# Cross-attention and a mixture of experts on one core: VectorE's order in attention, the top-four in wide operations, and an activation copy ahead of a sigmoid

## What is computed

```python
q = ctx @ Wq.T + bq; k = ctx @ Wk.T + bk
attention = softmax(q @ k.T)
x = x + layernorm(x) @ attention.T
h = layernorm(x)
top, idx = top_k(h @ gate_w.T + gate_b, 4)
weight = softmax(top)
gate = minimum(h @ w_gate[e] + b_gate[e], 7)
up = clip(h @ w_up[e] + b_up[e], -7, 7)
act = (up + 1) * gate * sigmoid(1.702 * gate)
x = x + sum(weight * (act @ w_down[e] + b_down[e]))
```

## Time and profile before

| | |
|---|---|
| median of 3 runs | 3115.03 us |
| the profiled execution | 3116.04 us, span 3113.9 us |
| TensorE matmuls busy | 2948.7 us, 95% of the span |
| VectorE busy | 1716.4 us, 55% |
| ScalarE busy | 1178.8 us, 38% |
| GpSimd busy | 563.5 us, 18% |
| mean granted TensorE clock | 0.984 of full speed |
| first gate product of the experts | 720.08 us |

### The profile page before, as it was taken

The page is one execution under the profiler, slowest core; times in us unless marked ns, Lnnn a source line. Parts: engine busy times, 40 slices in busy tenths (PEclk is TensorE's granted clock), DMA queues, the critical chain, the costliest instruction groups (busy, mean ns, idle before and its releaser), DMA issues.

```text
span 3113.9 us, 44999 instructions
## 1 busy us (share of the span) xinstructions
PE 2948.7 (95%) x14948; PEld 1512.9 (49%) x14949; DVE 1716.4 (55%) x2856; ACT 1178.8 (38%) x1235; POOL 563.5 (18%) x502
## 2 busy tenths in 40 slices
PE   6798988987999999999999999999999999999997
PEld 2354545553544455544445444454445444445443
DVE  3687878674454544555544555555555544553532
ACT  2332323233343433444433434444343433442422
POOL 1032322331111111111111111111111111111111
PEclk8899999988999999999999999999999999999999
DMA  6776656556554655755655756575565555565333
GB/s 192 175 182 176 176 151 174 181 159 207 158 162 101 178 140 144 220 162 159 191 141 143 224 148 195 162 227 151 151 200 155 162 157 160 155 178 139 75 66 61
DMA packets 343541, 501.38 MB, mean 161 GB/s; under 512 B 190881, under 2 KB 190881, under 8 KB 343234
## 3 DMA queue, kind: packets, MB, share of 16 engines
q0 software_dynamic: 45856, 152.33, 22.2%
q10 hardware_dynamic: 94576, 225.46, 20.4%
q1 hardware_dynamic: 203058, 122.94, 15.0%
HBM read 354.64 MB, written 112.46 MB: 150 GB/s over the span
## 4 chain that ended last, share of the span: by engine, by line
PE 75%; DVE 1%; ACT 0%; issue 0%; DMA 0%; ACTq 0%; POOL 0%; SPq 0%; POOLq 0%
PE psY L1291 24%; PE psG L1269 21%; PE psU L1269 21%; PE psX L1275 4%; PE psG L1327 3%; PE psA L1282 2%; DVE gt L1219 0%; ACT aT L1134 0%; DVE gt L1222 0%; DMA acc<-y,idxs 0%; DMA idxs<-slots 0%; ACT xT L1130 0%; ACTq L1056 0%; POOL acc L1121 0%; ACTq L1028 0%
## 5 line engine op out<-in xcount | busy, mean ns | idle before, releaser
L1291 PE MATMUL psY<-W,aT 128*128 128x512 f16 x3456 | 769.6, 379 | 23.5 <-ACT aT L1134 23.5
L1269 PE MATMUL psG<-W,xT 128*128 128x512 f16 x3072 | 686.5, 380 | 4.3 <-ACT xT L1130 4.3
L1269 PE MATMUL psU<-W,xT 128*128 128x512 f16 x3072 | 683.9, 379 | 0.0
L1291 PEld LDWEIGHTS psY<-W,aT 128*128 128x128 f16 x3456 | 336.9, 98 | 402.7 <-ACT aT L1134 27.5
L1269 PEld LDWEIGHTS psG<-W,xT 128*128 128x128 f16 x3072 | 300.5, 98 | 369.7 <-issue 9.1
L1269 PEld LDWEIGHTS psU<-W,xT 128*128 128x128 f16 x3072 | 300.6, 98 | 333.9
L1097 POOL DMA_INDIRECT acc<-y,idxs x143 | 225.3, 1575 | 1051.0 <-DVE y L1210 1008.0
L1210 DVE SCALAR_TENSOR_TENSOR y<-bias,idxs,y 128x1024 f32<-128x1024 f32 x143 | 183.7, 1285 | 389.3 <-ACT y L1141 389.3
L653 PE MATMUL psM<-W,XT 128*128 128x512 f16 x1392 | 355.9, 379 | 8.6 <-DVE xr L900 8.6
L1092 POOL DMA_INDIRECT xg<-xn_tab,idxg x145 | 156.8, 1082 | 953.1 <-PE psX L1275 902.8
L1141 ACT ACTIVATE y<-psY,idxs 128x1024 f32<-128x1024 f32 x143 | 159.2, 1114 | 438.1 <-DMA idxs<-slots 406.8
(11 more groups left out here) (157 smaller groups left out, 2634.3 us busy)
## 6 DMA issues: line engine op xcount, KB each, us to landing
stage_more<-in_L_ffn_w_down ACTq DMA_DIRECT2D x62, 1024.0 KB, 10.0
stage<-in_L_ffn_w_gate ACTq DMA_DIRECT2D x60, 1024.0 KB, 6.7
stage_more<-in_L_ffn_w_up ACTq DMA_DIRECT2D x31, 1024.0 KB, 5.6
stage<-in_L_ffn_w_up ACTq DMA_DIRECT2D x30, 1024.0 KB, 12.4
stage<-in_x SPq DMA_DIRECT2D x32, 512.0 KB, 5.4
xr<-in_x SPq DMA_DIRECT2D x32, 512.0 KB, 4.7
acc<-xr SPq DMA_DIRECT2D x32, 512.0 KB, 3.8
xn_tab<-x2h SPq DMA_DIRECT2D x32, 512.0 KB, 3.0
```

Source lines behind the costliest of these rows:

```text
L1269: op = pe.matmul(ps[:], xT[:, k, :, a], weights(par, c, offset + k * I, I), start=k == 0 and n == 0, stop=k == KH - 1 and n == 2)
L1291: op = pe.matmul(psY[:, h * HALF:(h + 1) * HALF], aT[:, k, :, a], weights(par, c, 2 * KH * I + k * H + h * HALF, HALF), start=k == 0 and n ...
```

## The change

On VectorE, LN2 is split: its statistics stay behind the residual sum, its normalisation goes behind the next step's maximum and negation. LN1's reciprocal and scale go ahead of its normalisation. In the first batch the low parts of a tile go behind the next tile's maximum, and the exponential waits for them. The four one-hot comparisons become one, the four multiply-and-sum instructions a product and a reduction, and the intermediate wt goes. On TensorE, LN2's transpositions and the logits come later in the product; the second batch's contexts and queries and keys are made in the first batch's steps, with two quarters in psQ and psR; later batches use psE first and psM after it, and wait for each apart. The start has wide copies, contexts in three PSUM buffers, and the context's load ahead of the gate weights'. In the experts the copy aT comes ahead of the sigmoid.

```diff
+        early = psM_halves + [psQ[:, :], psR[:, :]]
+        first_pairs = [psM, psE, psT, psM]
...
+        CTX_ALONE = range(NT // 2)
+        QK_ALONE = range(NT // 2, NT)
+        QK_ORDER = (0, 2, 1, 3)
...
+        def quarter(bk, n):
+            if batch(bk) == 0:
+                return (psM_halves + psE_halves)[n]
+            return early[n] if batch(bk) == 1 else (psE_halves + psM_halves)[n]
...
-            sp.dma_start(wqk_in[:, 0, :], g["Wq"]).then_inc(s_small, 16)
-            sp.dma_start(wqk_in[:, 1, :], g["Wk"]).then_inc(s_small, 16)
+            sp.dma_start(wqk_in[:, 0, :], g["Wq"]).then_inc(s_wqk, 16)
+            sp.dma_start(wqk_in[:, 1, :], g["Wk"]).then_inc(s_wqk, 16)
+            load_ctx(0)
...
-            load_ctx(0)
...
                 def exponent():
                     act.wait_ge(s_nmx, tile(b1, s + 1))
+                    act.wait_ge(s_alo, tile(b1, s))
...
+            pe.wait_ge(s_wqk, 16 * 2)
+            for n in range(2 * KC):
+                op = pe.transpose(psT[:, n * D:(n + 1) * D], wqk_in[:, n // KC, n % KC * P:(n % KC + 1) * P], ident[:])
+            op.then_inc(s_wT, 1)
+            pe.wait_ge(s_wTev, 1)
...
             def queries_and_keys(bk):
                 pe.wait_ge(s_cTev, per(NT // 2, bk, NT // 2))
                 for n in range(4):
+                    if n == 0 and not first(bk):
+                        pe.wait_ge(s_exp, NT * batch(bk))
+                    if n == 2 and not first(bk):
+                        pe.wait_ge(s_x2, NT * (batch(bk) - 1))
+                    one_quarter(bk, n)
...
-                held = range(10, 10 + KH)
+                held = range(16, 16 + KH)
...
-                    if 2 <= m < 2 + KH:
-                        logits_block(m - 2)
+                    if 4 <= m < 4 + KH:
+                        logits_block(m - 4)
...
+                if b1 is not None and b2 is None:
+                    if s == 0:
+                        pe.wait_ge(s_wTev, 2)
+                    if s in CTX_ALONE:
+                        if s > 0:
+                            pe.wait_ge(s_cTev, per(NT // 2, following(b1), s))
+                        context(following(b1), s)
+                    if s in QK_ALONE:
+                        n = QK_ORDER[s - QK_ALONE[0]]
+                        pe.wait_ge(s_cTev, per(NT // 2, following(b1), NT // 4 * (n % 2 + 1)))
+                        one_quarter(following(b1), n)
...
+            def second_norm(bt, n):
+                if n >= 1 or batch(bt) > 0:
+                    alone(dve, s_x2T, tile(bt, n), s_past)
+                normalise(1, xs2[:], xr[:, n % 2, :], s_xs2, tile(bt, n))
...
                     dve.tensor_scalar(nmx[:, 0:1], mx[:, 0:1], -1.0, None, ALU.mult).then_inc(s_nmx, 1)
+                    if b2 is None and s > 0:
+                        lo_parts(s - 1)
+                    if b2 is not None and s > 0:
+                        second_norm(*late)
                     dve.wait_ge(s_x1[s % 2], per(8 * NT, b1, 16 * (s // 2 + 1)))
-                    layernorm(0, xs[:], x1[:, s % 2, :], s_xs, tile(b1, s))
+                    statistics(0, x1[:, s % 2, :], tile(b1, s))
                     dve.wait_ge(s_exp, tile(b1, s + 1))
                     link(v, dve.reciprocal(sc[:, 1:2], psm[:, 0:1]))
                     dve.tensor_scalar(sc[:, 0:1], sc[:, 1:2], S_PROB, None, ALU.mult).then_inc(s_sc, 1)
+                    normalise(0, xs[:], x1[:, s % 2, :], s_xs, tile(b1, s))
...
-                    for k in range(TOPK):
-                        v.inc(dve.tensor_tensor_reduce(out=junk[:, k, :], in0=oh[:, j, k, :], in1=rk[:], scale=1.0, scalar=0.0,
-                                                       op0=ALU.mult, op1=ALU.add, accum_out=dest_f[:, k:k + 1]))
+                    link(v, dve.tensor_tensor(junk[:, :, :], oh[:, j], every_k(rk), ALU.mult))
+                    v.inc(dve.tensor_reduce(dest_f[:], junk[:, :, :], AX_X, ALU.add))
...
-                    for k in range(TOPK):
-                        v.inc(dve.tensor_scalar(oh[:, j, k, :], iota_e[:], i4[:, k:k + 1], None, ALU.is_equal))
-                    dve.wait_ge(v.sem, v.now())
+                    link(v, dve.tensor_tensor(oh[:, j], every_k(iota_e),
+                                              i4[:, :].rearrange("p (k o) -> p k o", o=1).to_broadcast([P, TOPK, E]), ALU.is_equal))
...
-                    layernorm(1, xs2[:], xr[:, s % 2, :], s_xs2, tile(b2, s))
+                    statistics(1, xr[:, s % 2, :], tile(b2, s))
+                    if b1 is None or s == NT - 1 or own is False:
+                        second_norm(b2, s)
...
+                guarded(act, prev_guard, lambda: evac_a(i - 1))
                 act.wait_ge(s_gmin, i + 1)
                 act.activation(sg[:], gt[:], ACT.Sigmoid, scale=ALPHA).then_inc(s_sig, 1)
-                guarded(act, prev_guard, lambda: evac_a(i - 1))
```

More of the change, by code:

```diff
@@ L515, in prepare @@
                     context((0, 0), pair)
+                act.wait_ge(s_wT, 2)
+                act.activation(gateT[:, :, :].rearrange("p k e -> p (k e)"), psT[:, 0:KH * E], ACT.Copy).then_inc(s_wTev, 1)
                 act.wait_ge(s_padout, 16 * 5)
@@ L551, in step @@
                     guarded(act, own, exponent)
-                    if b2 is None and s - 1 in CTX_STEPS:
-                        context(following(b1), s - 1 - CTX_STEPS[0])
+                    if b2 is None and s - 1 in CTX_ALONE:
+                        context(following(b1), s - 1)
                 if late:
@@ L622, in context, with one_quarter @@
                     alone(pe, s_ctx, per(16, bk, 16), s_past)
+                ps = first_pairs[pair] if first(bk) else psT
                 for t in range(2):
                     for c in range(KC):
-                        op = pe.transpose(psT[:, t * HALF + c * P:t * HALF + (c + 1) * P],
+                        op = pe.transpose(ps[:, t * HALF + c * P:t * HALF + (c + 1) * P],
                                           cx[:, 2 * pair + t, c * P:(c + 1) * P], ident[:])
                 op.then_inc(s_cT, 1)
+            def one_quarter(bk, n):
+                for c in range(KC):
+                    op = pe.matmul(quarter(bk, n), WT[:, n // 2, c, :], cxT[:, c, n % 2 * HALF:(n % 2 + 1) * HALF],
+                                   start=c == 0, stop=c == KC - 1)
+                op.then_inc(s_qk, 1)
             def queries_and_keys(bk):
@@ L632, in queries_and_keys, with first_energies @@
                 for n in range(4):
-                    for c in range(KC):
-                        op = pe.matmul(quarter[n], WT[:, n // 2, c, :], cxT[:, c, n % 2 * HALF:(n % 2 + 1) * HALF],
-                                       start=c == 0, stop=c == KC - 1)
-                    op.then_inc(s_qk, 1)
+                    if n == 0 and not first(bk):
[3 more added lines that the diff above has]
+                    one_quarter(bk, n)
+            def first_energies(bk):
                 pe.wait_ge(s_qkev, per(4, bk, 4))
@@ L762, in step @@
                     if s == NT - 1:
-                        def next_batch():
-                            alone(pe, s_exp, tile(b1, NT), s_past)
-                            if b2 is not None:
-                                alone(pe, s_x2, tile(b2, NT), s_past)
-                            queries_and_keys(following(b1))
-                        guarded(pe, more, next_batch)
+                        pe.wait_ge(s_exp, tile(b1, NT))
+                        first_energies(following(b1))
                 if late:
@@ L790, in link, with every_k, statistics @@
                 dve.wait_ge(tally.sem, tally.now())
-            def layernorm(which, out, src, ready, n):
+            def every_k(row):
+                return row[:, :].rearrange("p (o e) -> p o e", o=1).to_broadcast([P, TOPK, E])
+            def statistics(which, src, n):
                 v = Tally(s_ln[which], n * 3)
@@ L876, in step @@
                     alone(dve, s_pack, tile(bt, n + 1), s_past)
-                    assert v.n == 11
-                if b1 is not None:
+                    assert v.n == 7 + 1
+                if b1 is not None and (b2 is not None or s == NT - 1):
                     guarded(dve, own, lo_parts)
```

85 lines of the change are left out of this document (36 added, 49 removed).

## The result

The changed kernel takes 3031.53 us (median of 4 runs, 3028.04 to 3032.38); the kernel before took 3115.53 beside it (4 runs). The ratio of the mean times is 0.9727, with a 95% interval of 0.971 to 0.9744: faster by 84 us. The forecast was 3032, its range 3017 to 3057. The profiled execution took 3032.38 us, its span is 3030.6, so 83.3 us less than the span before.

What follows compares the result with a forecast made beforehand. VectorE was taken to bound attention's steady step, TensorE the experts. Terms 28.4 + 0.5 + 6.7 + 16.9 + 7.9 + 0.5 + 21.8 = 82.7 us gave 3033.3 for the profiled execution, hence 3032 us; range 3017 to 3057.

Steps and rivals of the forecast that it cites:

- What bounds the step: Attention's steady step: VectorE sets it at 17.52 us a round, and TensorE has 1.5 us of room.
- Sum of the step: Steady step: VectorE's savings together −1.44 us, round 16.08; taken as 20 intervals of 1.42, 28.4 us.
- TensorE must follow: Steady step: TensorE's round without idling is 16.02 us with a context transposition, so the step was taken as 16.1.
- The rival in which TensorE becomes the bound: Steady step: xs2 and x2T both arrive late, the step stays at 16.8 us; 3046 us, chance 0.14.
- Batch starts: Two later batch starts: queries and keys no longer pause for the residual sum; 6.7 us gained.
- First batch: First batch alone: shorter VectorE rounds and an earlier product after the last maximum; 16.9 us gained.
- Start: Program start: earlier context load and back-to-back transpositions bring the first energies to 36.3 us; 7.9 us gained.
- First product: First product to first residual sum: no term in the sum; DMA exposure of its second half put at no more than 2 us.
- cheaper VectorE work gives nothing there: Last batch: its steps are TensorE's, so no gain was counted there.
- Last tile: Last tile: its list of experts and slots is a chain of VectorE alone; 0.5 us gained.
- Experts: Expert loop: copy aT ahead of the sigmoid removes 16 half-tile waits of 1.36 us; 21.8 us gained.
- Wide instructions blocked: Rival: wide VectorE instructions lose 0.3 us each beside GpSimd's slot DMAs; 3044 us, chance 0.05.

Runs made afterwards that it cites:

- norm_late: Changed kernel with LN2's normalisation back directly behind its statistics, ahead of the maximum; 3043.29 us.
- recip_late: low_own with LN1's reciprocal and scale back behind LN1's normalisation; 3044.39 us.
- top4_narrow: Changed kernel with four one-hot comparisons and four multiply-and-sum instructions again instead of the wide forms; 3036.07 us.
- lean: Changed kernel with three VectorE instructions less in each tile's list (two casts and the separate token number); 3019.89 us.
- xr_wait: Changed kernel with the wait for the last residual sum put ahead of all queries and keys at the two later batch starts; 3036.96 us.
- low_own: Changed kernel with the low parts of the first batch back in their own step; 3026.93 us.
- qk_after: Changed kernel with the second batch's queries and keys computed after the first batch's last exponential, not in quarters beside its steps; 3037.85 us.
- warm: Changed kernel with twelve useless 128x512 float32 matmuls ahead of the second batch's first energies; 3029.59 us.
- lean_low_fill: Changed kernel with the edits of lean and low_own, and six useless float32 matmuls before the second batch's first energies; 3015.78 us.
- sigmoid_first: Changed kernel with the sigmoid ahead of the activation copy aT again in the expert loop; 3052.06 us.
- places_early: Changed kernel with TensorE's earlier places back: LN2's transpositions from the tenth matmul, logits from the second; 3037.32 us.
- ctx_last: Changed kernel with the first context load issued last of the small loads, as before the change; 3029.72 us.

## Why the prediction was right

The total was right to 0.5 us, and most steps with it. Two parts had the right size for another reason than given, and errors cancelled: 5.0 us more than summed (steady steps 2.8, experts 1.3, first batch 0.6, first interval 0.3) met 4.9 less (last xr to gate product 2.1, last batch 1.7, first product 1.0, batch starts 0.1).

- *What bounds the step*: right. norm_late, recip_late and top4_narrow each moved the step by what VectorE's instructions cost (0.72, 0.26, 0.32; predicted 0.69, 0.26, 0.30).
- *Sum of the step*: 1.56 instead of 1.42 to 1.44. wt gave 0.14 and not 0.19: from er to seen it is 280.89 − 280.23 = 0.66, before 339.91 − 339.11 = 0.80. Missed were 0.12 behind xr: LN2's statistics followed it after 1.47 us and now after 1.35, since the second semaphore wait between them is gone (in norm_late it stays gone). 0.72 + 0.26 + 0.32 + 0.14 + 0.12 = 1.56.
- *TensorE must follow*: right in kind. I put its round at 16.02 and the step at 16.1; lean shows 15.84. The rival in which TensorE becomes the bound was 0.12 us from deciding.
- *Batch starts*: right to 0.1 us, and xr_wait brings the cost back.
- *First batch*: the size was right (17.5 for 16.9), the reason wrong. The step that failed is "the low parts of a step move behind the next maximum, so VectorE no longer waits for ah: 8.52 − 1.30 − 0.26": I gave the 1.30 to the low parts' move. low_own and recip_late show that the reciprocal's move, which I had priced at 0.26 alone, is enough to take it away. Beside it the low parts' move does only what I had listed as its price, a 1.28 us instruction in the exponential's way, and costs 2.7 us net. The quarters beside it were priced about right (qk_after: 8.4, predicted 7.5). Inside the part two errors cancelled: the seven rounds took 48.4 us for 50.2, since the two with a quarter came to 6.9 and not 7.7 (the four before them, taken at 7.5 or 7.8 at the lower clock, took 7.80, 6.92, 7.79 and 7.29), and the last maximum to the product took 15.8 for 14.7, its energies being at the lower clock.
- *Start*: 7.9 as predicted, by other terms. "the first transposition starts near 12.4" failed: the context landed at 14.45. The four groups of transpositions and the copy behind them took 7.06 us and not 8.9, and gave 1.8 of the 2.05 back; that the two errors met is luck. From there to the energies it took 14.8, as taken (15.0). By the rule that the array starts throttled and activity releases it (the Trainium skill, TensorE: Matmul & The Clock Gate, Part 1: The HAM clock gate) the unbroken run should speed up, and the trace agrees: 1.94, 1.91, 1.59, 1.04 us for four equal groups, where in the kernel before, with 1.11 us of idling between them, all four took 1.94 to 1.97.
- *First product*: not in the sum. It began at the lower clock after 6.33 us of idling, 1.0 us. warm shows the cause, and the other profiles bear it out: in all ten of the changed kernel and its variants that idle 5.4 to 6.7 us there, the energies take 3.49 to 3.75 us, and in warm, lean_low_fill and qk_after, which idle 0.84 us at most, 1.88 to 1.98. But the higher clock alone would not have given the 1.0 back. In sigmoid_first, places_early and lean the product ran at the higher clock, and its second half waited 0.80, 1.26 and 1.34 us for the transposed ah, so that it took 11.6 to 12.1 us to the first xr all the same. This is the exposure that the prediction had put at no more than 2 us and left out of the sum. In lean:

```profile
107.22 5.34 PE L676 MATMUL psM<-W,XT 128*128 128x512 f16 x24 [1.34 <-DMA W<-ah]
```

- *Last batch, "cheaper VectorE work gives nothing there"*: in this profile it lost 1.7. TensorE's clock was lower in the first half of its first product. Windows of 4 us (length, busy us and count, then granted clock, DMA share, GB/s), TensorE around that product, changed kernel:

```profile
502.00:506.00 4.00, 2.69 (x15) 1.00 0.83 206
506.00:510.00 4.00, 3.50 (x11) 0.64 1.10 192
```

and before, busy us of TensorE, its weight loads, VectorE, ScalarE and GpSimd:

```profile
566.00:570.00 4.00, 1.52 (x10) 0.75 (x8) 3.46 (x14) 0.39 (x2) 3.08 (x4) 1.00 0.88 152
570.00:574.00 4.00, 4.00 (x20) 1.85 (x19) 2.42 (x5) 0.62 (x1) 0.57 (x2) 1.00 1.03 243
```

TensorE idled less ahead of it than before, and yet the granted clock fell. Of the 14 profiles five have this interval at 16.2 to 16.3 us (the changed kernel, norm_late, top4_narrow, ctx_last, warm) and nine at 14.5. So with nearly the same instructions around it, it varies from profile to profile. Whether the change makes the longer one more likely isn't shown: the kernel before has one profile.
- *Last tile*: −1.6 instead of 0.5. From the last xr to the first gate product it took 42.2 us, in the twelve experiments 39.8 to 41.3, before 40.6. The first rows' copy xT was late in this execution (the gate product starts 6.5 us after the rows' transpositions began, elsewhere 4.9 to 5.9); the 0.5 can't be seen in that spread.
- *Experts*: 23.1 for 21.8. sigmoid_first confirms the mechanism; the term was 16 pieces of 1.36, whereas 23.5 − 1.4 = 22.1 of waiting went. The last 1.0 I can't assign.
- *Wide instructions blocked*: fell. The comparison takes 291 to 294 ns in all 32 tiles, within a slot DMA's issue or outside. The SBUF — State Buffer page of the Trainium skill (Who interferes with whom) would have the comparison wait for a GpSimd instruction that reads SBUF. The same section adds, as inferred, that generating a DMA's descriptors needs GpSimd's write interface and a tensor_tensor takes only the read one; the trace agrees with that, and whether the issue reads SBUF at all no run here shows.

## What to carry to other kernels

When a wait goes away, ask which of several simultaneous moves released it, and undo them one at a time: here two 0.15 us instructions were worth 1.5 us a round, and beside them the large move made for the same wait cost time. An engine that follows with a tenth of a microsecond of room is already the next bound, so take its own round (busy with no idle) before pricing more savings. Effects of 1 to 2 us at a clock transition or a landing differ between executions; look at the same interval in several profiles before explaining one.

## What the runs showed of the hardware

- Equal groups of transpositions ran at 1.94, 1.91, 1.59 and 1.04 us at the program's start, though the granted clock of those windows is listed as 1.00: the durations tell the level there, the column does not.
- Ahead of the last batch's first product, where TensorE's longest idle piece in the changed kernel is 1.31 us, the clock fell in five of 14 profiles and not in the others. Idling 5.4 to 6.7 us before the second batch's energies went with the lower clock in all ten profiles, and useless matmuls in its place kept it up in both that had them.
- A comparison of float32 with uint32 indices, and a sum of 128 float32 columns into uint32, take 0.29 us on VectorE, as their float32 forms do.
- A float32 128x512 matmul shows as two records and takes 0.87 us at the higher clock (twelve took 10.46 in warm), a float16 one about 0.22 (48 took 10.52).
- The narrow comparisons had single instructions of up to 481 ns where their median is 237 (top4_narrow). The two groups of four that took longer than 0.68 us, 0.73 and 0.89, lie wholly within the issues of slot DMAs:

```profile
L931 DVE TENSOR_SCALAR oh<-iota_e,i x128: 232/237/481, 127.8 to 637.7; 128x32 f32<-128x32 f32 x128
```

What those waited for was not tried.
